# One fused attention and routed-FFN kernel: DVE's order of small steps, the order of first loads, and scores one pair ahead

## The reference

```
x = x + xattn(layernorm(x), ctx, ctx)      # 16 heads of 16; blocks of 64; every block pair but a few
x = x + ffn(layernorm(x))

def ffn(xf):
    e = argmax(softmax(xf @ gate_w.T))     # one of two experts for each token
    routed = relu(xf @ w1[e] + b1[e]) @ w2[e] + b2[e]
    shared = relu(xf @ sw1 + sb1) @ sw2 + sb2
    return routed + shared                 # hidden size 1024
```

## Time and profile before

| what | value |
|---|---|
| three runs | 934.51, 938.26, 942.17 us; median 938.26 |
| the profiled execution | 933.05 us, span 931.1 us |
| PE busy | 797.0 us (86%) |
| DVE, ACT, POOL busy | 600.2, 486.1, 422.9 us |
| mean granted TensorE clock | 0.944 of full speed |

### The profile page before, as it was taken

One profiled execution on the slowest core, in us unless ns is written; L12 is line 12 of the kernel. 1 busy time (PEld: TensorE's weight loads), 2 busy tenths in 40 slices (PEclk: granted clock), 3 DMA queues, 4 the chain that ended last, 5 costly groups with the idle time before them and its releaser, 6 DMA issues.

```text
span 931.1 us, 24363 instructions
## 1 busy us (share of the span) xinstructions
PE 797.0 (86%) x8374; PEld 680.0 (73%) x8374; DVE 600.2 (64%) x1242; ACT 486.1 (52%) x1124; POOL 422.9 (45%) x773
## 2 busy tenths in 40 slices
PE   3366877789898999999999989899999999989894
PEld 3345666577877878786868787787878687868794
DVE  5656467676858586867777675858586776745331
ACT  3363534537465555556464646555464647365452
POOL 5543423424446263737364453627373544455311
PEclk8586989999999999999999999999999999999998
DMA  8666231344536353444444453534433544414630
GB/s 282 168 173 235 80 103 48 99 139 133 164 115 193 96 154 124 138 157 122 148 147 134 141 164 113 192 92 147 134 117 132 157 137 139 144 47 148 224 106 23
DMA packets 97387, 128.19 MB, mean 138 GB/s; under 512 B 14655, under 2 KB 82623, under 8 KB 97088
## 3 DMA queue, kind: packets, MB, share of 16 engines
q1 hardware_dynamic: 89760, 107.89, 37.7%
q0 software_dynamic: 6624, 18.95, 6.2%
q10 hardware_dynamic: 960, 0.79, 0.4%
HBM read 90.80 MB, written 37.04 MB: 137 GB/s over the span
## 4 chain that ended last, share of the span: by engine, by line
PE 55%; DVE 18%; DMA 12%; issue 6%; ACT 4%; POOL 2%; SPq 1%; DVEq 1%; ACTq 1%; POOLq 0%
PE acc L724 15%; PE hid L535 12%; PE nd L638 9%; PE work L535 5%; DVE nmax L1178 5%; DVE T L1197 4%; DMA scratch_q<-T 4%; PE work L622 3%; DVE T L1194 3%; PE work L666 2%; PE work L544 2%; PE work L591 1%; PE nd L591 1%; DMA QP<-scratch_m 1%; PE work L652 1%
## 5 line engine op out<-in xcount | busy, mean ns | idle before, releaser
L1456 POOL TENSOR_TENSOR hl<-h,hh 128x256 fp32r<-128x256 f32 x228 | 166.0, 733 | 328.4 <-ACT hh L981 328.0
L1197 DVE RECIPROCAL T<-nd 128x256 f32<-128x256 f32 x64 | 112.3, 1755 | 55.9 <-PE nd L638 50.9
L981 ACT ACTIVATE h<-hid,bias 128x256 f32<-128x256 f32 x144 | 69.0, 479 | 103.7 <-PE hid L535 103.7
L535 PE MATMUL hid<-Xs,W 128*128 128x256 f32 x816 | 113.7, 295 | 1.1
L724 PE MATMUL acc<-w_hi,hh 128*128 128x256 f32 (+1 forms) x528 | 114.1, 298 | 0.0
L965 ACT ACTIVATE PT<-work 128x512 f32<-128x512 f32 x192 | 99.8, 593 | 24.1 <-PE work L622 22.6
L1178 DVE TENSOR_REDUCE nmax<-work 128x8 f32<-128x512 f32 x128 | 82.2, 684 | 45.1 <-PE work L591 44.8
L535 PEld LDWEIGHTS hid<-Xs,W 128*128 128x128 f32 x816 | 107.7, 203 | 4.1 <-issue 3.1
L724 PE MATMUL acc<-w_lo,hh 128*128 128x256 f32 (+1 forms) x528 | 106.6, 284 | 0.0
L535 PE MATMUL hid<-Xr,W 128*128 128x256 f32 x768 | 104.4, 285 | 0.0
L535 PEld LDWEIGHTS hid<-Xr,W 128*128 128x128 f32 x768 | 94.2, 188 | 4.7 <-DVE Xr L1131 0.2
(11 more groups left out here) (191 smaller groups left out, 1620.1 us busy)
## 6 DMA issues: line engine op xcount, KB each, us to landing
W<-w1q SPq DMA_DIRECT2D x64, 512.0 KB, 6.1
KP<-scratch_k SPq DMA_DIRECT2D x192, 64.0 KB, 2.5
QP<-scratch_q SPq DMA_DIRECT2D x180, 64.0 KB, 2.3
scratch_k<-T SPq DMA_DIRECT2D x16, 512.0 KB, 3.5
scratch_q<-T SPq DMA_DIRECT2D x16, 512.0 KB, 3.2
yt<-yq SPq DMA_DIRECT2D x17, 260.0 KB, 2.8
xt<-xq SPq DMA_DIRECT2D x17, 256.0 KB, 3.8
xin<-x SPq DMA_DIRECT2D x16, 256.0 KB, 3.5
```

The costliest lines, as they stand in the source:

```text
L535: mm = nc.tensor.matmul(dst, R(s), R(m), start=n == 0, stop=n == len(steps) - 1)
L981: last = nc.scalar.activation(dst, hid[:, u % 2, a, :], ACT.Relu, bias=bias[:, 2 * u + a:2 * u + a + 1])
L1197: nc.vector.reciprocal(T[:, p, :], nd[:, p % 2, 1, :]).then_inc(sem["inverted"], 1)
L1456: nc.gpsimd.tensor_tensor(R(hl[:, u % 2, a]), h32[:, u % 2, a], hh[:, u % 2, a], ALU.subtract).then_inc(sem["hl_done"], 1)
```

## The change

- Tile iterations, DVE: the second gate pair, move_ids, the mask, finish_tile and norm1_apply leave the end of the iteration. They come in the next one between the maxima: behind maxima 4 to 7 finish_tile, the gate pair, move_ids and the mask; behind maxima 8 to 11 norm1_apply. rank_tokens goes behind maximum 13.
- PE: ranks goes from ahead of visit 2 to ahead of visit 3; visit(i+1, 0) goes ahead of tile_up(m, 3). GUESSED gets pair 6 as well.
- Iterations 0 to 2: transposed scores are made one pair ahead of the values, exponentials likewise, and table_relu goes behind pair 6.
- Start: the nine constants go behind the spreads of K, the piece loads behind the bounce of Q; ACT's first split_high go behind spread_q and front_v; DVE takes norm 1 of sequence 1 and maxima 0 to 3 ahead of its wait for the constants. There are five slots for all pieces, none in PT, and DVE makes the low part of every odd piece under 14.
- POOL's last two splits go behind the reciprocal deviation of norm 2.
- Tail: for the last tile bsel is sent ahead of the wait for the queued tokens.

```diff
-GUESSED_EARLY, GUESSED = (1, 3, 5, 7), (1, 3, 5, 7)
+GUESSED_EARLY, GUESSED = (1, 3, 5, 7), (1, 3, 5, 6, 7)
...
-STAGES, LATE_STAGES = 7, 3
-SLOTS = [n % STAGES for n in range(2 * STAGES)]
-SLOTS += [n % LATE_STAGES for n in range(W1_PIECES + W2_PIECES - len(SLOTS))]
+STAGES, BY_VECTOR = 5, 14
+SLOTS = [n % STAGES for n in range(W1_PIECES + W2_PIECES)]
...
 # SP, load_tile
-                    if u == 0:
+                    if u == 0 and not at:
                         sp.wait_ge(sem["x_queued"], 32 * (m + 1))
                         load_tile_x(m, row)
...
                 sp.dma_start(bsel[:, :], b1[:, bass.ds(HT * expert + HT, HT)]).then_inc(sem["bias_loaded"], 16)
+                if at:
+                    sp.wait_ge(sem["x_queued"], 32 * (m + 1))
+                    load_tile_x(m, row)
...
 # SP, start: the nine constants
             for half in range(2):
                 spread_k(half)
+            sp.wait_ge(sem["proj_lo"], 4)
+            for dst, src in ((bias1[:, :], b1), (bsum[:, :], blocksum), (hsum[:, :, :], headsum),
...
+                sp.dma_start(dst, src).then_inc(sem["consts_loaded"], 16)
...
 # PE, iteration
                     shared_up(n, 1)
-                    ranks(n, claim(i, ("rk", 0), tile=tile))
                 visit(i, 2, more)
                 if shared:
                     shared_down(n, 0)
                     shared_up(n, 2)
+                    ranks(n, claim(i, ("rk", 0), tile=tile))
                 visit(i, 3, more)
...
+                if not tile:
+                    scores_t(i, 0, more)
+                for p in range(0 if tile else PAIRS):
+                    if p % 2:
+                        fill(n, m, tile, (p + 1) // 2, expert)
+                    if p + 1 < PAIRS:
+                        scores_t(i, p + 1, more)
+                    values(i, p)
...
                 attention_out(i, more)
+                if more:
+                    visit(i + 1, 0)
                 if tile:
                     tile_up(m, 3)
-                if more:
-                    visit(i + 1, 0)
...
 # DVE, iteration
                 for v in range(1, VISITS):
                     for j in range(4 * v, 4 * v + 4):
                         maximum(i, j)
+                        if shared and j == 13:
+                            rank_tokens(n)
                     splits(i, v + 1)
+                    if v == 1 and (type(i) is not int or i > 3):
+                        finish_tile(m - 1)
                     if shared and v == 1:
-                        rank_tokens(n)
+                        gate_scores(n, 1)
+                        if type(i) is not int or i > 1:
+                            move_ids(n - 1)
+                        choose(n)
+                    if shared and more and v == 2:
+                        norm1_apply(i + 1)
...
                 gate_scores(i, 0)
                 shared_low(i)
-                gate_scores(i, 1)
-                if shared:
+                if not more:
+                    gate_scores(i, 1)
                     move_ids(n)
-                choose(i)
-                if tile and more:
-                    finish_tile(m)
+                    choose(i)
                 if shared and not tile:
                     level_sum(n)
-                if norm1:
-                    norm1_apply(i + 2)
...
 # DVE, start
+            norm1_stats(1)
+            norm1_apply(1)
+            for j in range(4):
+                maximum(0, j)
+            dve.wait_ge(sem["consts_loaded"], 16 * 9)
...
 # POOL
-                for k in range(3 if shared else 5, 11):
+                for k in range(3 if shared else 5, 10):
                     splits(i, k)
...
                 reciprocal_deviation(i, 1)
+                splits(i, 10)
...
+            reciprocal_deviation(1, 0)
+            pool.wait_ge(sem["first_q_bounced"], 16)
+            for n in range(STAGES):
                 load(n)
```

More of the change, by code:

```diff
@@ L219, in stage @@
         def stage(n, like):
-            s = (h32[:, 0], h32[:, 1], yp[:, :, :], *(PT[:, k] for k in range(4)))[SLOTS[n]]
+            s = (h32[:, 0], h32[:, 1], yp[:, :, :], yt[:, :, :], xt[:, :, :])[SLOTS[n]]
             return flat(s)[:, 0:512].rearrange("p (a b) -> p a b", a=2)
@@ L228, in by_vector @@
         def by_vector(n):
-            return n % 2 == 1 and n < 2 * STAGES
+            return n % 2 == 1 and n < BY_VECTOR
         def low_done(n):
@@ L450, in _ @@
             sp.dma_start(x1[:, 0, :], indicator).then_inc(sem["indicator_loaded"], 16)
[L451 to L457, removed]
             load_x(1)
@@ L603, in maxima @@
             def maxima(i):
+                if type(i) is int and i == 0:
+                    pe.wait_ge(sem["consts_read"], 1)
                 bank = claim(i, ("mT", 0))
@@ L829, in iteration @@
                     shared_up(n, 3)
-                for group in range(GROUPS):
+                if not tile:
[6 more added lines that the diff above has]
+                    values(i, p)
+                for group in range(GROUPS if tile else 0):
                     scores_t(i, 2 * group, more)
@@ L876, in _ @@
             iteration(0, False, False, True)
-            pe.wait_ge(*low_done(2 * STAGES - 1))
+            pe.wait_ge(*low_done(BY_VECTOR - 1))
             pe.wait_ge(*low_done(len(pieces) - 1))
@@ L1047, in iteration @@
                     shared_relu(n, UNITS - 1)
[L1048 to L1051, removed]
+                if not tile:
+                    exps(i, 0)
+                    exps(i, 1)
+                for p in range(0 if tile else PAIRS):
+                    if p == 2:
+                        splits(i, 7)
+                    if p == 5:
+                        splits(i, 8)
+                    if p + 1 < PAIRS:
+                        exps(i, 2 * p + 2)
+                        exps(i, 2 * p + 3)
+                    if p in guessed(i):
+                        guess_inverse(i, p)
+                    if shared and p == 6:
+                        table_relu(i - 1)
+                for group in range(GROUPS if tile else 0):
                     for j in range(4):
@@ L1055, in iteration @@
                         tile_relu(m, group)
[L1056 to L1062, removed]
+                    for p in (2 * group, 2 * group + 1):
+                        if p in guessed(i):
+                            guess_inverse(i, p)
                 splits(i, 9)
@@ L1091, in _ @@
             projection_high(3)
-            for n in range(EARLY_PIECES):
-                split_high(n)
             act.wait_ge(sem["first_q_bounced"], 16)
@@ L1099, in _ @@
             front_v(0, acc[:, :, :])
+            for n in range(EARLY_PIECES):
+                split_high(n)
             iteration(0, False, False, True)
@@ L1388, in _ @@
                 .then_inc(sem["consts_read"], 1)
-            norm1_stats(1)
             for n in range(EARLY_PIECES):
@@ L1392, in _ @@
                     split_low(n)
-            norm1_apply(1)
-            for j in range(4):
-                maximum(0, j)
             splits(0, 1)
@@ L1618, in _ @@
             context_low(0)
-            pool.wait_ge(sem["zeroed"], 3)
-            for n in range(LATE_STAGES + 2):
-                load(n)
             nc.gpsimd.memset(V[:, :, :, :], 0.0).then_inc(sem["zeroed"], 1)
@@ L1630, in _ @@
                 nc.gpsimd.memset(level_row[r:r + 1, :], 1.0).then_inc(sem["zeroed"], 1)
-            for n in range(LATE_STAGES + 2, STAGES):
+            reciprocal_deviation(1, 0)
+            pool.wait_ge(sem["first_q_bounced"], 16)
+            for n in range(STAGES):
                 load(n)
-            reciprocal_deviation(1, 0)
             for n in range(EARLY_PIECES):
```

11 lines of the change are left out of this document (6 added, 5 removed).

## The result

The changed kernel takes 940.31 us in the median of 20 runs, the kernel before 936.33 in as many; the ratio is 1.0053 with a 95% interval of 1.0031 to 1.0076. So it is slower, by 4.0 us in the medians (5.0 by the ratio) where +10.8 was forecast: outside measurement noise and within the 1% that I had named as "no change". The profiled execution has a span of 935.0 us against 931.1.

A forecast was written before the change was run, and what follows sets the result against it. PE bounds the kernel, busy 797.0 of 931.1 us. Terms -3.2 - 2.85 - 1.15 + 20.4 + 0.6 - 3.0 = +10.8 on the median 938.26 give 949, chance 0.55; range 896 to 960.

The forecast's parts named there:

- part 1: DVE's new order in a tile iteration: waits of 1.21 go, visit 3 loses 2.9, so +1.7 an iteration.
- the second: Tile iteration: gate pair held to the end of POOL's run, ending at 607.14 instead of 603.84 alone.
- rival B: Gate products get in between POOL's operations, one behind each hl; the loop stands still, 926 us; chance 0.13.
- The term of +20.4: The twelve tile iterations: +1.7 us each from the mask coming late for visit 3.
- My one row: Profile row of T, 0.42 alone, taking 1.49 inside a POOL run; taken as the model for the gate's hold.
- Pair 6 at 0: Tile iterations: guessing pair 6 leaves PE's wait for pair 7's T; 0, or at best -1.1.
- Start: Up to the first transpose of the maxima: bounce of Q at most -2.9, later maxima against it; taken as +2.5.
- Iteration 0: Scores one pair ahead, -3.7, and a shorter wait at norm 2, -2.0.
- The last piece: Iteration 0's norm 2 wait of 6.29: rstd goes ahead of POOL's last two splits; -2.0, from -5.5 to 0.
- The pairs: Iteration 0, scores one pair ahead: pairs fall from 17.6 to 13.8 at DVE's own pace, -3.7.
- Iterations 1 and 2: Table wait and most waits for exps go, bounded by Q's spread: -2.85 each, with a new wait of +1.7 in iteration 2.
- Tail: Last routed tile: bsel sent first shortens the 4.22 wait by 3.0, between -1 and -4.2.

The follow-up runs named there:

- the first test: Without the kernel's work: POOL runs two or four subtractions, DVE a pair of operations beside them; T's pair takes 1.39, or 0.76 with one input from PSUM.
- the kernel before with the sending first: The kernel before with POOL's sending of a finished tile's rows moved ahead of the two tile_hidden, nothing else; 0.9853 of the kernel before.
- both tests: Two tests of POOL beside DVE without the kernel's work: subtractions alone, then an indirect DMA issue and two subtractions; in the second T takes 0.88.
- the changed kernel with the sending first: The changed kernel with POOL's sending of a finished tile's rows moved ahead of the two tile_hidden, nothing else; 0.9723 of the kernel before.
- the two kernels with the gate moved as well: The changed kernel with sending ahead of tile_hidden and gate products behind shared_low, 897.7 us; the same plus later order, constants first and later splits, 889.75 us.

## Why the prediction was wrong

The hold of POOL on the gate was there, but its size was not, and a part that I had put at nothing was not nothing. That the kernel came out slower all the same, and inside the range, is luck: the loop measured +2.5 for +20.4, while the start and iterations 0 to 2 together, forecast at -7.2, measured +3.8. With those as forecast, it would have come out some 7 us faster.

- *The step that failed* is in part 1: "I take the second, since that row is of the same kind and length", that is, the gate pair held to the end of POOL's run. It was held by one POOL operation each. The mask came 2.2 us behind yt, not 4.5, and visit 3 lost 0.62 with up to 0.9 around it, where I had 2.9. That is rival B, whose price for the loop was 0 and which I gave 0.13. The term of +20.4 measured +2.5. The page SBUF — State Buffer of the Trainium skill, section "SBUF: two separate sides", says that of a DVE operation with two SBUF inputs and a GpSimd operation the one that starts first gets the shared pair of ports for its whole instruction; a hold over several instructions is not in it. Here the first test agrees, with DVE's product ending 0.28 behind the POOL operation that ran. My one row, with 1.49 over two operations, was true of that place in the kernel and of no other that the tests reached.
- *Pair 6 at 0.* I looked only at DVE's time and at T's end. The guess leaves DVE a product on two SBUF tiles beside POOL's DMA issue, which then takes 1.20 for 0.96; hl and so T come 0.2 later, and with the clock's falls the loop is 11.0 us longer with the guess (608.48) than without (597.45). So the loop's +2.5 is a sum of two: the rest of the change with pair 6 divided is worth -8.5 (605.97 to 597.45; some 5 of it at the same clock, the rest by four falls for six), and the guess takes that back.
- *Start.* +2.5 was taken between -2.9 and +5; +4.4 in the pair of profiles. The bounces did fall to 2.9 us and the spreads landed 3 us sooner, and DVE stood 4.26 for the constants. The term was inside its bounds there, but the true size is uncertain: 47.78 is the earliest of the eight runs with the changed start, and the old start's first transpose came at 43.36 in the one profile and at 46.49 in the other (the kernel before with the sending first).
- *Iteration 0.* -5.7 forecast, -3.3 measured in the pair. The last piece was right: norm 2's wait went from 6.29 to 4.14 (forecast -2.0), and half of what is left is norm 2's scaling of 0.73 taking 2.60 beside the two splits that had been put there. The pairs fell by 1.2 instead of 3.7: three T products met POOL's splits and took 0.71 to 1.27.
- *Iterations 1 and 2.* -4.0 forecast, +2.7 measured. The wait at the table went, and one for the spread of Q (1.45) came, as I had bounded it; but I carried the new order's price into iteration 2 alone, and only as a wait for POOL. With the old order they take 105.45, where 101.9 was forecast without the new wait; and the kernel before with the sending first, whose iterations 1 and 2 are the old ones, took 105.43. So no run shows a gain of the size forecast there.
- *Tail.* -3.0 for bsel: the 4.22 became 1.52, and 2.70 for the tile's tokens, now sent last, stand in front of it: as much together. The last stretch still lost 2.4, as forecast for it and iteration 15 together, but not by this; one part that shows is a wait of 0.99 for the tokens of the tile after it, which is gone. The rest was not traced.

The upper half of the range and the 0.55 on the forecast rested on a single row read as a rule.

## What to carry to other kernels

Ahead of moving a step of DVE, list by operands which of its operations have two inputs in SBUF, and lay POOL's busy runs beside the new place: here 1.5 us an iteration hung on two products that stood beside four hl, and a swap of two POOL steps was worth more than the whole reordering. A row that shows a hold gives its size for that place only; ask what a hold of one operation and one of the whole run would each make of the time, and give the nearer mechanism its full chance. A guess isn't free because the engine that makes it has room: look at the products that it leaves to DVE, and at what of POOL they then stand beside. And a loop's sum in one profile can hide the clock: compare iterations at the same granted clock, and count the others.

## What was not expected of the hardware

- DVE and POOL alternate: with both busy on SBUF inputs, a DVE product of 0.42 took 0.94 and POOL's subtraction 0.90 instead of 0.72, turn by turn. A scaling with one SBUF input also waited (0.81 for 0.28); a form with one input in PSUM never did (0.42).
- An indirect DMA issue on POOL (0.99) held such DVE products too, if they came in its later part: one that started 0.61 ahead of the issue's end took 0.98, one that started in its first 0.05 took 0.43. And it is held itself: 1.20 for 0.96 in the kernel, where such a product had begun 0.06 ahead of it.
- Why pair 7's T is held over two POOL operations in the kernel (1.47 to 1.86 in every tile iteration, before and after the change), and over one in both tests, stays open.
- The granted clock: about 3 us at the lower level (1.2 GHz) came in four to twelve of the twelve tile iterations where a PE wait of 1.5 to 1.8 for T was left, in half of them where T was free but waits of 0.54 and 0.69 stood in visit 2 (the kernel before with the sending first), in none where T was free and 0.65 and 0.71 were left (the changed kernel with the sending first), and in the first alone in the two kernels with the gate moved as well. With pair 6 divided, one fall began just behind the wait for T, from 443.5 on. What tells an iteration that falls from one that doesn't was not settled.
